# Four z tiles behind the first scan, rounding tails by pairs, and convolution tiles by halves, in a one-core hybrid layer

## The reference, cut to what matters

```
x = x + attention(layernorm(x))          # 16 heads of 16, causal, rotary
x = x + ffn(layernorm(x))                # fp6 rounding in blocks of 32, 256x256 product, bias
x = x + mamba_and_mlp(layernorm(x))      # below
x = x + ffn(layernorm(x))                # the same rounding and product again

# mamba_mixer(rmsnorm(x)):
xp, z = split(x @ in_proj_w.T)           # 512 columns each
xc = silu(causal conv of 4 taps over xp + conv_b)
dt, B, C = xc @ x_proj_w.T               # 16 + 16 + 16 columns
dt = softplus(dt @ dt_proj_w.T + dt_proj_b)
h = h * exp(dt * A) + (dt * u) * B       # 16 states, over 1024 steps
y = (h . C) + xc * D
out = (y * silu(z)) @ out_proj_w.T
```

## Time and profile before

| what | us |
|---|---|
| median of three runs | 9492.4 |
| lowest, highest | 9489.47, 9493.67 |
| the profiled execution | 9479.75 |
| its span, first to last instruction | 9477.6 |
| mean granted clock of TensorE | 0.956 |
| busy PE, DVE, ACT, POOL | 7914.4, 7518.7, 4325.4, 4192.9 |

### The profile page before, as it was taken

One profiled execution on the slowest core, in us unless ns is written; L12 is line 12 of the kernel. 1 busy time (PEld: TensorE's weight loads), 2 busy tenths in 40 slices (PEclk: granted clock), 3 DMA queues, 4 the chain that ended last, 5 costly groups with the idle time before them and its releaser, 6 DMA issues. The chain is left out here.

```text
span 9477.6 us, 102293 instructions
## 1 busy us (share of the span) xinstructions
PE 7914.4 (84%) x33684; PEld 4015.1 (42%) x33684; DVE 7518.7 (79%) x11589; ACT 4325.4 (46%) x8247; POOL 4192.9 (44%) x2633
## 2 busy tenths in 40 slices
PE   5788797887978879788887988879888797887978
PEld 2344353443434434354343544435344353443534
DVE  5787978879688796877878778797787977879777
ACT  2535445354452644525445354453534535355353
POOL 1451815518154271632716336172461724518155
PEclk8999999999999999999999999999999999989999
DMA  3010020200202002020020200102011020100202
GB/s 81 1 43 13 5 50 1 54 1 5 51 1 54 1 9 46 0 54 1 13 42 0 55 1 23 33 0 55 1 27 28 0 55 1 39 17 5 51 1 54
DMA packets 265207, 230.19 MB, mean 24 GB/s; under 512 B 26947, under 2 KB 237635, under 8 KB 264531
## 3 DMA queue, kind: packets, MB, share of 16 engines
q1 hardware_dynamic: 264678, 223.50, 10.8%
HBM read 151.60 MB, written 70.25 MB: 23 GB/s over the span
## 5 line engine op out<-in xcount | busy, mean ns | idle before, releaser
L665 POOL TENSOR_TENSOR arena<-arena 128x1024 f32<-128x1024 f32 x1024 | 2435.1, 2388 | 1182.5 <-DVE arena L1080 775.4
L813 ACT ACTIVATE PS<-arena,Aneg 128x512 f32<-128x512 f32 x2048 | 1411.9, 691 | 1656.6 <-DVE XNT L1120 931.0
L731 ACT ACTIVATE arena<-PS 128x512 f32<-128x512 f32 (+3 forms) x3072 | 1285.5, 510 | 859.9 <-PE PS L1315 854.9
L986 DVE TENSOR_REDUCE pm<-PS 128x1 f32<-128x512 f32 (+3 forms) x1728 | 1050.2, 663 | 274.4 <-PE PS L1294 175.4
L1439 PE MATMUL PS<-XNT,identf 128*128 128x512 f32 x2048 | 985.4, 604 | 309.9 <-POOL XNT L648 309.9
L627 POOL TENSOR_SCALAR_AFFINE_SELECT arena<-arena 128x512 f32<-128x512 f32 x512 | 328.1, 641 | 2058.1 <-ACT arena L731 2058.1
L1291 PE MATMUL PS<-arena 96*128 96x512 bf16 (+3 forms) x3072 | 1087.3, 377 | 126.0 <-PEq L1523 52.8
L1439 PE MATMUL PS<-arena,identf 128*128 128x512 f32 x2048 | 996.0, 609 | 163.9 <-DVE arena L1096 163.9
L1315 PE MATMUL PS<-arena 99*128 99x512 bf16 (+3 forms) x3072 | 888.5, 330 | 5.5
L1424 PE MATMUL PS<-arena,sel 96*128 96x512 bf16 x1664 | 504.3, 385 | 405.6 <-DVE arena L1096 335.9
L1327 PE MATMUL PS<-arena 128*32 128x512 f32 (+3 forms) x6144 | 651.3, 497 | 40.3 <-ACT arena L738 35.7
(11 more groups left out here) (150 smaller groups left out, 13495.7 us busy)
## 6 DMA issues: line engine op xcount, KB each, us to landing
pieces_scratch<-arena SPq DMA_DIRECT2D x816, 64.0 KB
arena<-pieces_scratch SPq DMA_DIRECT2D x68, 384.0 KB, 9.1
arena<-pieces_scratch SPq DMA_DIRECT2D x85, 256.0 KB, 9.4
arena<-in_x SPq DMA_DIRECT2D x17, 1024.0 KB, 5.7
U<-in_x SPq DMA_DIRECT2D x17, 1024.0 KB, 5.6
arena<-pieces_scratch SPq DMA_DIRECT2D x136, 128.0 KB, 9.3
out<-X SPq DMA_DIRECT2D x64, 256.0 KB, 13.3
arena<-pieces_scratch SPq DMA_DIRECT2D x17, 768.0 KB
```

Source lines behind the costliest of these rows:

```text
L665: nc.gpsimd.tensor_tensor(DB[:, n % 2], DTU[:, j, half(th)].unsqueeze(1).to_broadcast([P, SP2, TH]), BB[:, SP2 * sg:SP2 * (sg + 1), :], AL ...
L731: A(PT[s % len(PT)][:, hh, 0:w], bank(t_bank(n))[:, 0:w], ACT.Exp, scale=DH ** -0.5)\
L813: A(bank(da_bank(m)), DT[:, j, half(th)], ACT.Exp, scale=Aneg[:, j, SP2 * sg + ss:SP2 * sg + ss + 1]).then_inc(S("dA"), 1)
L986: V_.tensor_reduce(out=dst, in_=bank(r % 3)[:, 0:share * w].rearrange("p (h w) -> p h w", h=share), op=ALU.max, axis=AX.X, negate=True).th ...
```

## The change

What it does, edit by edit:

- The tanh of a z tile is written to Z itself instead of TZ, and z tiles 0 to 5 have banks 0 to 5, tiles 6 and 7 banks 0 and 1. The order is 0, 1, 2, 3, 6, 7, 4, 5. The last four have their tanh and gate inside scan units 0 (tiles 6, 7) and 1 (tiles 4, 5).
- In `quant_products` the row products of a pair follow the pair's turn; the last pair is turned before its bias products. That pair's multiplication by the scales goes from POOL to VectorE.
- The joint rows' last pair is turned after the first in_proj tile.
- Convolution tiles 0 and 1 get first term and taps by halves; the fourth gets its taps, tanh and gate by halves. x_proj's order is interleaved, with the first dt_proj in it.
- The relus come in front of the B and C pieces, the gates of z tiles 0 to 3 between relu 1 and relu 2. The pieces of half 1 come after the first dt u product. The first B pair needs only half 0's pieces.
- B pair 1 is copied by ScalarE between the first two exponentials of unit 0. POOL's dt addition for tile 1 comes behind its product of unit 0.
- The dummy products among x_proj and those of units 0 and 1 go, but for two (four instructions) in unit 1.

```diff
-            return k % 4 if k < 4 else (k + 2) % 4
+            return k if k < 6 else k - 6
...
-        DT_BANK = (6, 7, 0, 1, 2, 3, 6, 7)
+        DT_BANK = (6, 7, 6, 7, 0, 1, 2, 3)
...
+                if n == 0:
+                    add_dt(1)
...
             tanh_z(0)
             tanh_z(1)
-            tanh_c(ND - 1)
+            tanh_c(ND - 1, half(0))
             tanh_z(2)
             tanh_z(3)
...
+            x_rows(0)
+            tanh_c(ND - 1, half(1), last=1)
+            absolute(0)
+            x_rows(1)
+            for n in range(1, ND):
+                absolute(n)
+            exponential(0)
+            for n in range(ND, ND * NTH):
+                absolute(n)
+            exponential(1)
...
-            spread_b(0)
             for th in range(NTH):
                 own.wait(own.n - NTH + 1 + th)
                 A(DT[:, :, half(th)], DT[:, :, half(th)], ACT.Ln, bias=1.0).then_inc(S("dtl"), 1)
-            for k in range(4, ND * NTH):
-                tanh_z(k)
+                if th == 0:
+                    spread_b(0)
...
+                    if m == 0:
+                        spread_b(1)
+                if n < 2:
+                    for k in Z_LATE[n]:
+                        tanh_z(k)
...
+                last = NT // 2 - 1
+                if last in pairs:
+                    dve.wait_ge(S("q"), NT // 2 * (f + 1))
+                    V_.tensor_tensor(quant_place(f, last, 0).rearrange("p (n q) -> p n q", q=QB),
+                                     quant_place(f, last, 1).rearrange("p (n q) -> p n q", q=QB),
+                                     sc[:, last, :].unsqueeze(2).to_broadcast([P, 2 * NQB, QB]), ALU.mult)\
+                        .then_inc(S("xl"), 1)
...
+            for m in range(2):
+                for th in range(NTH):
+                    dve.wait_ge(S("conv0"), NTH * m + th + 1)
+                    taps(m, th * TH, TH)
+            silu_c(0)
+            dve.wait_ge(S("conv0"), 5)
+            taps(2, 0, T)
+            silu_c(1)
+
+            dve.wait_ge(S("conv0"), 6)
+            taps(ND - 1, 0, TH)
+            silu_c(ND - 2)
+            silu_c(ND - 1, half(0))
+            taps(ND - 1, TH, TH)
+            silu_c(ND - 1, half(1), last=1)
+            relu(0)
+            relu(1)
+            for k in range(4):
+                silu_z(k)
+            relu(2)
+            relu(3)
+            for n in range(ND, ND * NTH):
+                relu(n)
+            pieces_bc(0)
...
             times_u(0)
-            for k in range(4, ND * NTH):
-                silu_z(k)
-            dve.wait_ge(S("z"), ND * NTH)
+            pieces_bc(1)
...
+                if n < 2:
+                    for k in Z_LATE[n]:
+                        silu_z(k)
...
+                for p in range(NT // 2):
+                    if p == NT // 4:
                         keep_busy(row_bank((1, 3)[f], NT // NTH), (8, 11)[f])
...
+                    if last:
+                        pe.wait_ge(S("xl"), f + 1)
...
+                    if last:
+                        bias_rows(f, (2 * p, 2 * p + 1))
+                    if p:
+                        rows((1, 3)[f], wd, xt, NC, rnd=rnd,
+                             which=range(2 * p, 2 * p + 2) if p > 1 else range(NT // NTH))
...
+            turn_joint(range(3))
...
                 in_proj(n)
+                if n == 0:
+                    turn_joint([3])
...
+            x_proj(0, 0)
+            x_proj(0, 1)
+            x_proj(1, 0)
+            x_proj(0, 2)
+            x_proj(0, 3)
+            x_proj(1, 1)
+            dt_proj(0)
+            x_proj(1, 2)
+            x_proj(1, 3)
+            for n in range(1, ND * NTH):
+                dt_proj(n)
...
-            pe.wait_ge(S("bc"), NTH)
+            pe.wait_ge(S("drl"), ND * NTH)
+            pe.wait_ge(S("bc"), 1)
+            spread_b(0)
+            for k in (6, 7, 4, 5):
+                if k in (4, 5):
+                    pe.wait_ge(S("bc"), k - 3)
+                in_proj(ND * NTH + k)
+            spread_b(1)
+            pe.wait_ge(S("bc"), NTH)
...
-                    if n < 2:
-                        keep_busy(5, (6, 2)[n])
                     if b_copied(n + 1):
                         spread_b(b_copied(n + 1))
                     if n == 1:
-                        keep_busy(5, 4)
+                        pe.wait_ge(S("z"), ND * NTH)
+                        keep_busy(5, 2)
                     if spread_c(n):
+                        if n == 0:
+                            pe.wait_ge(S("z"), 6)
```

More of the change, by code:

```diff
@@ L655, in pool_program @@
                     pool.wait_ge(S("Be"), th * NSG + sg + 1)
[L656 to L662, removed]
+                if sg == 2 and jt and jt + 1 < NJT:
+                    add_dt(jt + 1)
                 if n >= 2:
@@ L751, in tanh_z, with tanh_c, x_rows, absolute @@
             def tanh_z(k):
[L752 to L759, removed]
+                act.wait_ge(S("ip"), ND * NTH + Z_ORDER.index(k) + 1)
+                A(Z[:, k // NTH, half(k % NTH)], bank(z_bank(k)), ACT.Tanh).then_inc(S("tz"), 1)
+            def tanh_c(m, t=slice(0, T), last=0):
+                act.wait_ge(S("convd"), (2, 4, 5, 6)[m] + last)
+                A(TC[:, m, t], XC[:, m, t], ACT.Tanh).then_inc(S("tc"), 1)
+            def x_rows(th):
+                act.wait_ge(S("xpr"), th + 1)
+                A(DTR[0:DR, half(th)], bank(4 + th)[SR:SR + DR, :], ACT.Copy)
+                A(BCP[:, half(th)], bank(4 + th)[0:SR, :], ACT.Copy).then_inc(S("bca"), 1)
+            def absolute(n):
+                th, j = divmod(n, ND)
+                act.wait_ge(S("dtp"), n + 1)
+                A(DT[:, j, half(th)], bank(DT_BANK[n]), ACT.Abs, bias=dtb[:, j:j + 1]).then_inc(S("dab"), 1)
+            def exponential(th):
+                act.wait_ge(S("dab"), ND * (th + 1))
+                own.did(A(DT[:, :, half(th)], DT[:, :, half(th)], ACT.Exp, scale=-1.0))
             for m in range(ND):
@@ L773, in scalar_program @@
             tanh_z(1)
-            tanh_c(ND - 1)
+            tanh_c(ND - 1, half(0))
             tanh_z(2)
             tanh_z(3)
-            for th in range(NTH):
-                act.wait_ge(S("xpr"), th + 1)
-                A(DTR[0:DR, half(th)], bank(4 + th)[SR:SR + DR, :], ACT.Copy)
-                A(BCP[:, half(th)], bank(4 + th)[0:SR, :], ACT.Copy).then_inc(S("bca"), 1)
-            for n in range(ND * NTH):
-                th, j = divmod(n, ND)
-                act.wait_ge(S("dtp"), n + 1)
-                A(DT[:, j, half(th)], bank(DT_BANK[n]), ACT.Abs, bias=dtb[:, j:j + 1]).then_inc(S("dab"), 1)
-                if j == ND - 1:
-                    act.wait_ge(S("dab"), ND * (th + 1))
-                    own.did(A(DT[:, :, half(th)], DT[:, :, half(th)], ACT.Exp, scale=-1.0))
+            x_rows(0)
[8 more added lines that the diff above has]
+            exponential(1)
             def spread_b(k):
@@ L1063, in vector_program, with relu @@
                     .then_inc(S("bc"), 1)
-            for n in range(ND * NTH):
+            def relu(n):
                 th, j = divmod(n, ND)
@@ L1270, in quant_products @@
                 rnd = (1, 4)[f]
[L1271 to L1272 removed]
+                for p in range(NT // 2):
+                    if p == NT // 4:
                         keep_busy(row_bank((1, 3)[f], NT // NTH), (8, 11)[f])
[L1274 removed]
+                    last = p == NT // 2 - 1
+                    if not last:
                         bias_rows(f, (2 * p, 2 * p + 1))
[L1276 to L1277 removed]
+                    if last:
+                        pe.wait_ge(S("xl"), f + 1)
+                    turn(rnd, lambda p, tt: quant_rows(f, p)[:, tt, :], "xd",
+                         lambda p: f * (NT // 2 - 1) + min(p + 1, NT // 2 - 1), [p])
+                    if last:
[3 more added lines that the diff above has]
+                             which=range(2 * p, 2 * p + 2) if p > 1 else range(NT // NTH))
             turned = maxima = 0
```

100 lines of the change are left out of this document (46 added, 54 removed), and 2 rows, old and new, of the table names.

## The result

The change makes the kernel slower: 9624.7 us (median of four runs, 9614.77 to 9632.78) against 9492.6 (9489.47 to 9493.67), a ratio of 1.0142 with an interval of 1.013 to 1.0155. The forecast was 9519 and its range ended at 9550. The profiled execution took 9632.78 for a span of 9630.8 at a mean granted clock of 0.937 (before 9479.75, 9477.6, 0.956). Runs of one kernel differ by up to 18 us, so I read what an edit does from stretches of the batch more than from totals.

What follows compares the result with a forecast made beforehand. One core runs 16 batches in sequence; the chain to POOL's fifth product was taken to set each. Per batch -2.05 + 2.0 + 1.7 = +1.65, x 16 = +26 on the 9492.4 median: 9519 us, range 9457 to 9550.

Steps and rivals of the forecast that it cites:

- the fifth product: POOL's fifth product in the scan's first units, at 967.45 before; every edit was carried to it, nothing priced behind.
- Rounding tails: Pair-by-pair order in the two rounding tails: last add 0.8 us later for f = 0, 0 for f = 1.
- The joint turn: Mixer's front: last joint turn behind the first in_proj puts the second in_proj 1.4 us later.
- (a): TensorE's 5.0 us pause before B pair 0 lowers the clock, 1.7 us lost; with (b) taken as 2.0 a batch.
- (b): Half 1's pieces on VectorE wait beside POOL's first product, delaying the fourth in_proj 0.9 us; overlaps (a).
- the rule: Shared SBUF port locked for whole instructions, casts included: pieces end at 951.4, and (b) alone takes back 1.85.
- (c): With fewer dummies, TensorE starts its list behind the eighth z gate at 1.2 GHz: +1.7 us a batch.
- The gain: Fifth POOL product at 965.4 against 967.45, z gates and their wait gone before the first scan: -2.05 a batch.

Runs made afterwards that it cites:

- e1_pad: The changed kernel plus one always-met wait on TensorE behind each scan unit's y product; 9562.39 us.
- e3_tails: The kernel before with only the change's rounding tails (products pair by pair, last pair scaled on VectorE); 9496.94 us.
- e4_before_pad: The kernel before plus three always-met waits on TensorE behind each scan unit's y product; 9513.39 us.
- e5_before_pad6: The kernel before plus six always-met waits on TensorE behind each scan unit's y product; 9549.34 us.
- e11_oldjoint: e10 with the last joint turn again in front of the first in_proj; 9445.77 us, ratio to before 0.9958.
- e6_gap: e2_pieces plus ten dummy products in TensorE's pause in front of the first B pair; 9508.45 us.
- e2_pieces: The changed kernel with half 1's B and C pieces in front of the first dt u product; 9601.85 us.
- e7_gapscan: e6_gap plus four and two dummy products in front of B pairs 2 and 3; 9482.95 us.
- e10: e7_gapscan with both rounding tails as in the kernel before; 9475.39 us, ratio to before 0.9985.
- e12: e11_oldjoint with the last four z tiles' tanh and gates in front of the first scan; 9430.94 us, ratio to before 0.9939.

## Why the prediction was wrong

The direction was right, the size was not: +1.65 a batch forecast, +9.67 measured.

- **The step that failed** is the sentence "behind it the order and the engines are those of before". It let me stop at the fifth product. There the changed kernel is 0.80 - 0.77 + 3.32 = 3.35 late, where +1.65 was forecast; the other 6.3 arise elsewhere, 4.6 of them in the jump at the end of a batch, which the sum put at nothing without a reason. Fewer instructions were counted nowhere as an effect, and e1_pad shows that they are one. Nothing in the trace before shows a slow jump, but the fetches of code are in it, and the length of the program was in the diff.
- **The attention, +1.40.** Before, 14 of 16 batches take 143.4 and two 145.3; after, it is two and 14. The difference in these two kernels is a low clock on the turns behind the last PV product. Two windows of after, and at the same place before:

```profile
866.00:868.00 2.00, 2.00 (x10) 1.70 (x10) 0.00 (x0) 0.88 (x2) 0.00 (x0) 0.52 0.00 0
868.00:870.00 2.00, 2.00 (x11) 1.81 (x10) 0.00 (x0) 1.33 (x3) 0.00 (x0) 0.63 0.03 8
```

```profile
856.00:858.00 2.00, 1.66 (x14) 1.38 (x15) 0.00 (x0) 1.11 (x3) 0.00 (x0) 1.00 0.00 0
858.00:860.00 2.00, 2.00 (x13) 1.80 (x12) 0.42 (x1) 1.06 (x2) 0.00 (x0) 1.00 0.04 8
```

  The code there is the same. Every variant has between 7 and 15 batches over 144, even e3_tails (9), e4_before_pad (12) and e5_before_pad6 (15). The prediction said that the batches of before meet the clock in the same way each time and that a new pace need not; it gave this no price. Its price was 0.4 to 1.4 us a batch in the variants. What decides a batch's state was not isolated.
- **Rounding tails** (+0.8 and 0): measured +0.80 in after, +0.75 in the median batch of e3_tails: right. For f = 1 the 0.15 fits the 0, but by luck: the prediction left the last add where it was, and it comes 1.9 earlier in e3_tails (2.3 in after), while the slower issue of the output DMA takes most of that back.
- **The joint turn**: second in_proj 3.11 behind the first (forecast 3.05), pieces of half 0 done 45.6 behind the joint rows (45.35). Right in the sum; but the moved turn was priced as hidden behind the convolution, and it costs 0.89 there by e11_oldjoint.
- **(a) and (b), the pause and the pieces, +2.0**: 1.48 by e6_gap and 1.35 by e2_pieces (the mean over two kinds of batches), 2.8 together. The rows gave 0.9 for the pieces. The Trainium skill, "SBUF — State Buffer", section "SBUF: two separate sides", has casts wait for POOL as well; the trace agrees (0.42 becomes 2.08 and 1.39, and each cast ends 0.3 behind the POOL instruction beside it). The pieces took 4.9 in all (958.48 to 963.40); the rule gave 4.0, since I had counted POOL's first product and not its dt addition behind it, the rows alone 3.1. Of this 1.35 reached the fifth product, between the rows' 0.9 and the rule's 1.85.
- **(c), the clock behind the z gates, +1.7**: 2.04 by e7_gapscan. Past the fifth product, where I did not look, 0.8 more is lost up to the 17th; the third fall, from 985, is part of it (42.6 with it, 42.2 in the two batches of after that have a shorter and later one, 41.8 before). The rest of the scan gave 0.35 back.
- **The gain, -2.05**: with both clock losses and the cast wait removed, 0.79 - 0.77 - 1.55 = -1.5 is left. But no edit earns the 1.55, the late order least of all: the term set a chain with a full clock against the 967.45 of before, which has the low clock of the earlier trace rows in it. With the clock held the order of before takes 24.44 (e3_tails) and the late order 24.42 (e7_gapscan), so 1.68 of the gain is that clock loss. With it taken out, tail and front cancel (+0.8, -0.77) and the change is worth nothing up to the fifth product. z early is 1.0 better than both with the clock held. I had priced the removed gates (2.70 and a wait of 2.29) as pure gain and charged the same gates inside the scan only for their own time, on the ground that VectorE is not the bound there. With four gates more it is.

Of the 106 us by which the forecast missed, the jump is some 70 (4.6 in each of 15 jumps; e1_pad gave back 62). Without it the changed kernel takes 9562 (e1_pad), still over the range's end, through the attention (+1.4 a batch) and the terms that were each too small (1.2 in (a) to (c), 0.5 in the gain, 0.4 behind the fifth product).

## What to carry to other kernels

Where a loop's body gets longer or shorter by some instructions, look at the jump at its end (time from the barrier to the first instruction of each engine) before explaining the rest, and at the code fetch beside it; a few waits that are always met may be worth more than the edit. Work that is moved out of an engine's idle time in front of a chain into the chain must be laid against that engine's occupancy there, not against its occupancy before the move. When an edit opens a pause on TensorE, fill it first and judge the edit afterwards. And a gain measured against a stretch that has a low clock in it is not the order's gain: look for the same stretch with the clock held, in another batch or another variant.

## What the runs showed that I had not expected

- The branch that closes TensorE's loop took 0.36 or up to 8.5 us, by the length of the program; ScalarE's, VectorE's and POOL's never over 0.1.
- The jump of the loop ends about 1.5 us after the batch's last block of code has landed: beside the one at 1313.59 to 1317.71 the fetch of 16 KB started at 1314.75 and took 1.4. With the block landed 8 us ahead or more, the jump took 0.35 to 0.46.
- SyncE's issue of a batch's last output DMA takes 0.37 in most batches before and 1.2 to 3.8 after; why was not tried. It is over 1 us in many batches of e10 and e12 too, which have the old tails.
- The same code meets the low clock in some batches of a run and not in others: 24.4 or 25.6 for the same stretch in e7_gapscan, 24.4 or 26.1 in e3_tails.
